# GNN kernel on one Trainium2 core: GpSimd keeps the scores of one chunk behind every gather, without its wait for the cast

## What is computed

```python
def _attention_aggregate(h_proj, sender, receiver, attn_vec, num_nodes):
    h_sender = h_proj[sender]
    h_receiver = h_proj[receiver]
    e = einsum('ehd,hd->eh', h_sender, attn_vec[:, :HD]) + einsum('ehd,hd->eh', h_receiver, attn_vec[:, HD:])
    e = leaky_relu(e, 0.2)
    e_max = segment_max(e, receiver, num_segments=num_nodes)
    alpha = exp(e - e_max[receiver])
    alpha_sum = segment_sum(alpha, receiver, num_segments=num_nodes)
    alpha = alpha / (alpha_sum[receiver] + 1e-08)
    msg = h_sender * alpha[..., None]
    return segment_sum(msg, receiver, num_segments=num_nodes)
...
h_in = _attention_aggregate(h_proj, src, dst, a_in, n)
h_out = _attention_aggregate(h_proj, dst, src, a_out, n)
combined = h_self + h_in + h_out + bias        # then a layer norm
```

## Time and profile before

| | us |
|---|---|
| median of 3 runs | 4346.67 |
| the profiled execution, its own time | 4351.3 |
| span of the trace (first to last instruction) | 4349.5 |
| busy: PE / DVE / ACT / POOL | 2402.7 / 2404.7 / 837.7 / 1621.1 |
| POOL's gathers, first start | 1858.03 |
| POOL's gathers, last start | 3063.94 |

### The profile page before, as it was taken

The page is one execution under the profiler, slowest core; times in us unless marked ns, Lnnn a source line. Parts: engine busy times, 40 slices in busy tenths (PEclk is TensorE's granted clock), DMA queues, the critical chain, the costliest instruction groups (busy, mean ns, idle before and its releaser), DMA issues.

```text
span 4349.5 us, 54947 instructions
## 1 busy us (share of the span) xinstructions
PE 2402.7 (55%) x16100; PEld 1506.8 (35%) x16104; DVE 2404.7 (55%) x3420; ACT 837.7 (19%) x1390; POOL 1621.1 (37%) x1455
## 2 busy tenths in 40 slices
PE   1688777694989859410000000000796767996763
PEld 1234555442455434400000000000453665553663
DVE  8998888735120467500000000000799878999877
ACT  0494333201110120000000000000111542111542
POOL 6201333218777760066677677766100000000000
PEclk9899999997999979655555555555897599997597
DMA  1000111142534107143333433334300151000153
GB/s 55 0 0 27 45 45 41 63 154 59 161 73 96 24 8 160 28 106 97 103 104 105 98 104 99 105 103 97 28 0 0 51 177 47 0 0 0 37 175 99
DMA packets 195116, 301.54 MB, mean 69 GB/s; under 512 B 120540, under 2 KB 133818, under 8 KB 194922
## 3 DMA queue, kind: packets, MB, share of 16 engines
q1 hardware_dynamic: 138986, 175.88, 12.8%
q0 software_dynamic: 40512, 62.87, 8.2%
q10 hardware_dynamic: 15552, 61.94, 4.7%
HBM read 191.65 MB, written 88.01 MB: 64 GB/s over the span
## 4 chain that ended last, share of the span: by engine, by line
PE 40%; another core or an unknown queue 21%; DVE 19%; issue 14%; ACT 4%; DVEq 1%; DMA 0%; ACTq 0%; SPq 0%; PEldq 0%
PE PS L532 11%; PE PS L692 7%; PE PS L1101 6%; PE PS L879 5%; PE PS L1105 4%; ACT arena L508 3%; DVE arena L553 3%; PE PS L968 2%; DVE arena L1194 2%; DVE arena L1137 2%; PE PS L955 1%; PE PS L470 1%; DVE arena L368 1%; PE PS L1240 1%
## 5 line engine op out<-in xcount | busy, mean ns | idle before, releaser
L1137 DVE TENSOR_REDUCE arena<-PS 128x512 f32 (+1 forms) x864 | 532.4, 679 | 1156.0 <-remote 898.8
L1101 PE MATMUL PS<-big_id,arena 128*128 128x512 bf16 x864 | 356.9, 413 | 1137.3 <-issue 571.7
L1296 POOL DMA_INDIRECT arena<-T_att,idx x864 | 816.4, 945 | 395.2 <-issue 263.4
L532 PE MATMUL PS<-arena 128*128 128x400 f16 (+2 forms) x4320 | 772.8, 329 | 269.1 <-issue 114.0
L532 PEld LDWEIGHTS PS<-arena 128*128 128x128 f16 (+2 forms) x4320 | 520.8, 155 | 512.3 <-issue 349.3
L1472 POOL DMA_INDIRECT order<-arena x400 | 511.2, 1278 | 252.4 <-issue 252.4
L1101 PEld LDWEIGHTS PS<-big_id,arena 128*128 128x128 bf16 x864 | 83.8, 97 | 1280.4 <-DVE arena L1137 692.3
L553 DVE TENSOR_SCALAR arena<-arena 128x1600 f16<-128x1600 f16 x448 | 385.6, 904 | 64.5 <-PE PS L532 60.4
L1069 ACT COPY arena<-PS 12x1024 bf16<-12x1024 bf16 x108 | 108.1, 1001 | 1606.4 <-remote 926.2
L692 PE MATMUL PS<-arena 128*128 128x512 f16 (+1 forms) x1575 | 316.6, 361 | 95.5 <-issue 82.2
L1105 PE MATMUL PS<-arena,pick 128*128 128x128 bf16 x3456 | 356.7, 229 | 0.0
(11 more groups left out here) (254 smaller groups left out, 2876.7 us busy)
## 6 DMA issues: line engine op xcount, KB each, us to landing
spill<-arena SPq DMA_DIRECT2D x108, 560.0 KB
arena<-spill ACTq DMA_DIRECT2D x108, 560.0 KB, 3.6
arena<-A SPq DMA_DIRECT2D x50, 800.0 KB
A<-arena SPq DMA_DIRECT2D x50, 400.0 KB, 2.4
arena<-A SPq DMA_DIRECT2D x50, 400.0 KB
arena<-T_att,idx POOLq DMA_INDIRECT x864
order<-arena POOLq DMA_INDIRECT x400
T_att<-h SPq DMA_DIRECT2D x2, 1600.0 KB, 12.4
```

Source lines behind the costliest of these rows:

```text
L532: return t.matmul(where, lhsT, rhs, start=False, stop=True, skip_group_check=True)
L1101: t.matmul(PS[:, bank:bank + BANK], OHb[:, s, :], big_id[:, :].unsqueeze(1).to_broadcast([P, HEADS, P]), start=True, stop=False, skip_grou ...
L1137: v.tensor_reduce(cmax[d][:, :, bass.ds(i * SLOTS + half * GROUP + j, 1)].rearrange("p h k -> p (h k)"), PS[:, bank:bank + BANK].rearrange ...
L1296: p.indirect_dma_start(out=ring1[:, b, j, :], out_offset=None, in_=T_att[d][:, :], in_offset=bass.IndirectOffsetOnAxis(ap=idx[:, d, k:k + ...
```

## The change

Two edits. `KEEPS` goes from 1 to 8. The loop over `part` then puts one transfer and one cast in turn: behind transfer j of group n stands the cast of chunk j of group n-1, 12 columns wide instead of 96. There are 864 casts instead of 108, each adds 1 to `scores_here`, and the waits for it at lines 1061 and 1293 count eight times as far. The second edit removes the wait of line 1307, by which POOL's next instruction waited for its own cast. The waits for `landed1` and `spilled1` are as before, but the one for `landed1` now stands behind the first transfer of the next group, where it stood behind the eighth.

```diff
-        KEEPS = 1
+        KEEPS = GROUP
...
                 if part == 0:
                     p.wait_ge(landed1[b], 16 * GROUP * (n // RING1 + 1))
                 p.tensor_copy(sE[d][:, g:g + w, :], ring1[:, b, part * w:(part + 1) * w, D:]).then_inc(scores_here, 1)
-                p.wait_ge(scores_here, KEEPS * n + part + 1)
```

## The result

| | before | after |
|---|---|---|
| median, us | 4346.67 (3 runs) | 4275.86 (4 runs: 4273.23 to 4287.53) |
| the profiled execution, us | 4351.3 | 4274.76 |
| its span, us | 4349.5 | 4273.0 |
| POOL's gathers, first start to last end, us | 1206.9 | 1237.0 |
| reductions of `top` before the last gather's end | 80 | 212 |

The change makes the kernel 1.6% faster: 0.984, 95% interval 0.9827 to 0.9852.

The account below looks back on a forecast made before the run. It took PE's late news to DVE during POOL's gathers as the bound: +50 us for a longer gather phase, +5 for its end, -3 for more chunks, +52 on 4346.7, so 4399 us; range 4280 to 4510.

Parts of the forecast that it names:

- What bounds the kernel now: During POOL's 1207 us of gathers, PE's news reaches DVE late, about one chunk in 13 us; DVE does 80 chunks there.
- The casts: POOL's 864 casts of 12 columns in the gather phase: 205 ns each, from rows of 96 and 3200 columns.
- The gap behind them: POOL's idle time between a cast and the next gather: taken as 0.27 us.
- The wait for the landing: POOL's wait behind each group's first gather until the previous group has landed: 0.28 us a group.
- the end of the phase: Last gathers, where slow transfers keep POOL from running a group ahead: +5 us, at most 13 us.
- The late wake-ups: POOL's late resumption behind its own casts in the gather phase: removing the wait gives back 105 us.
- The step that failed: DVE under the lengthened gather phase: 4 more chunks at a constant 15 us each, -3 us.
- The path opens: Rival: wider gather spacing lets PE's signals reach DVE; 4152 us or less if wholly (0.11), 4340 us in part (0.07).
- twice as much, some 80 chunks: Partial case of The path opens: PE's news passes to DVE at double rate under the gathers, 4340 us, chance 0.07.
- the three signs of being wrong: Gathers 1.25 to 1.35 us apart; DVE reduction bursts before POOL is done; POOL's group-head pauses still over 1 us.
- Cheap casts: Rival: casts hide in the 0.30 us between gathers, a gain below 0.14 us net each; 4269 us at best, chance 0.21.
- Signals in the way: Rival: eight times as many POOL signals on a late path keep the 105 us, 4504 us or more, chance 0.10.

Follow-up runs that it names:

- e12: Kernel before with eight casts a group, each cast's wait kept, at the level with late signals: 3818.92 us, ratio 0.8773.
- e10: Changed kernel with each cast cut in two of 6 columns, no wait behind them, at the level without late signals: 3610.07 us, 1.0427 to the kernel before.
- e11: Kernel before with only the wait behind its one cast a group removed, at the level with late signals: 4351.74 us, ratio 1.0006.
- e1: Kernel before with eight casts a group, each cast's wait kept, at the level without late signals: 3596.64 us, ratio 1.0397.
- e16: Kernel with one cast a group and no wait, plus an empty signalling GpSimd instruction behind each gather, late signals: 4355.35 us, 1.0008 to the kernel before.
- e18: As e16, with 24 more empty instructions behind each gather, meant to space the gathers without casts; distance stayed 1.25 us: 4352.30 us, 1.0007 to the kernel before.
- e9: Changed kernel with every cast two gathers later, at the level without late signals: 3482.07 us, 1.0063 to the kernel before.
- e2: Kernel before with only the wait behind its one cast a group removed, at the level without late signals: 3451.17 us, ratio 0.9975.
- e15: Changed kernel with every cast cut in three of 4 columns (24 a group), at the level with late signals: 3679.44 us, 0.8460 to the kernel before.
- e7: The kernel of e2 run again, at the level without late signals: 3449.85 us, 0.9969 to the kernel before.

## Why the prediction was wrong

**What bounds the kernel now** was right. DVE hardly works in the phase because PE's news comes late, and each chunk that moves under it is worth 0.735 us: 132 of them make 97 of the 98.4 us.

**The casts.** 205 ns from the slope of two rows, 203 measured. **The gap behind them** was taken as 0.27 us, from a row with a wait in it, "though some of them may be the wait". It is 0.15 us without a wait and 0.27 with one (e12). Eight casts and gathers take 8 x 1.325 = 10.60 us and not 11.36: the forecast had 0.76 x 108 = 82 us too much.

**The wait for the landing**: 0.28 us forecast. Behind the first gather of a group the median distance is 1.65 for 1.33 us, 0.32 us. By the page of the Trainium skill that the prediction weighed (DMA: Bandwidth & Descriptors, Anatomy of one DMA), this wait would be 0; the trace does not agree, and the measured time was the one to take. But some landings take far longer, so that these waits sum up to 57 us and not 30. The last three before the last gather are 2.70, 3.44 and 5.11 us, 11 us where the forecast had 5 for **the end of the phase**. At the lower level they are as long (2.74, 3.30 and 4.76 us in e10), so they are no late news.

**The late wake-ups.** Removing the wait was to give 105 us back. e11 shows that without the wait they come at other instructions. In the changed kernel the gaps behind the casts sum up to 38 us beyond 0.15 each; eight of 1.50 us stand about 147 us apart, and e1 has eight as regular ones of 1.73 us at the lower level, so they are hardly late news, and 27 us are left. As e11 gained nothing, what shrank the late ones was not the wait's removal by itself; that it was the greater distance fits, and is not shown by a run of its own. The sum of the measured terms is 108 x 10.60 + 57 + 38 = 1240 us, for 1237. Errors of 82 us too much and of 60 too little (38 for the pauses, 22 for the landings with the end of the phase) mostly cancelled: +30 came for +55. That the length of the phase came out near is luck.

**The step that failed** is "55 us more of gathers let DVE take 4 more chunks at 15 us each: -3 us". It took 132 more, -97 us. The prediction held the rate of the path constant at one chunk in 13 to 15 us, though it depends on how densely POOL issues its gathers; in the changed kernel it is one in 1237 / 212 = 5.8 us. The rival *The path opens* said so, and named 1.42 to 1.46 us against 1.50 in the scatter phase as its ground. Its case "twice as much, some 80 chunks" is the nearest to what came, 132 chunks, but it had 4340 us for 4276, and got 0.07. What speaks for it is now measured: between 1.25 and 1.55 us the path goes from closed to open. The arguments against it did not bear: that a pause of 2.64 us lets no burst through tells of a single pause in a stream 1.25 us apart, not of a stream that is thinner throughout. And that a reduction starts inside a gather tells of DVE and the port, not of the path of the signals, so "new pauses would open nothing" did not follow. Had the gathers really stood 1.42 us apart throughout, as forecast, the kernel would by e12 have been near 3819 us, an estimate, and far below the range: the error in the gap kept the change from doing much more than it did, and so that the time lies only 4 us outside is luck too.

Two of the three signs of being wrong came: gathers 1.25 to 1.35 us apart (1.33), and bursts of reductions before POOL is done. The sign for the forecast by the mean, 1.42 to 1.46 us, came as well (1.43), but it is a mean of 1.33 and of long pauses.

**The rivals.** *Cheap casts* had the place right: the net price of a cast is 1.325 - 1.25 = 0.075 us, below its 0.14. By its formula the phase would then have been 108 x (8 x 1.215 + 7 x 0.075 + 0.485) = 1159 us; the pauses behind the casts and the long landing waits made it 1237. *Signals in the way* is out: e16 adds eight signals in a group and its time is that of the kernel before (1.0008, 0.9999 to 1.0018). That a memory port locked for a whole gather is the cause was argued against in the prediction; the burst of DVE under the gathers (2011.91 us) agrees with that.

**What stays open.** What sets the level: the kernel doesn't, and the chip doesn't; the two sets without late signals were those in which four kernels ran beside the one before, the six with them had one to three. That is an agreement in eight sets, and whether it is a cause was not tested. Whether the casts between the gathers matter beyond the time they take: e18 was to show it and did not, and the scatter phase speaks against it without settling it. What PE's signals, SP's register instructions and POOL's own instructions share, that all of them are late together, no view shows, so the mechanism behind the effect of the distance is unknown. And the changed kernel did not run at the level without late signals; e9, nearest to it, was 0.6% slower than the kernel before there, and the change would have the landing waits on top.

## What to carry to other kernels

When an engine gets the news of its producer late while another engine issues transfers back to back, the rate of that path is a variable of the change and not a constant: price first what a change does to the issuer's spacing. An edit that makes the issuer a little slower can pay off many times where the path is the bound (24 casts instead of one: 3679 for 4347 us), and costs where it isn't (8 casts: 3597 for 3459 us), so find out first which of the two the kernel is in, by the waits in its trace. Two edits that pull such a spacing in opposite directions are to be tried one at a time: here eight casts alone gave 12.3%, and with the wait removed as well 1.6 to 1.9% were left.

## What the runs showed of the hardware

- At the higher level, while GpSimd issues gathers 1.25 us apart, other engines' signals and SP's own register instructions are late: 31 of 106 of these took over 0.5 us between 2000 and 2400 us, up to 1.40 us, where 0.05 us is the most without late signals (e1, e2). Most of the late ones take near 0.70 or 1.40 us; of 970 bare signalling instructions of POOL in e16, 637 take 0.69 to 0.71 us.
- The effect is steep in the spacing: 77 to 80, 166 to 212, 512 to 552 and 840 chunks at 1.25, 1.33, 1.43 and 1.55 us. A scatter 1.49 us apart shows none of it.
- The kernel before ran on one chip at 4345 and at 3462 us. DVE has waits ended by an unnamed source under the gathers in every trace at the first level (56 us at the widest spacing, e15), and none in the eight traces at the second, not even with gathers 1.25 us apart (e2, e7).
- A wait for the engine's own last instruction costs POOL 0.12 us even when nothing is late: 0.27 us behind a cast with it (e1), 0.15 without (e10).
- A cast of 12 columns takes 0.20 us, two of 6 in a row 0.32, one of 96 0.28: nearly all of it is fixed.
